# Macaron block (two mixture-of-experts layers around a selective scan): second expert layer of an older group in the first half of an iteration, first layer of a younger group in the second half

## The chip, the core and the metric

The kernel runs on one core of a Trainium2 chip. The metric is the device time of one execution in microseconds (us). The engines are PE (TensorE, matrix products), DVE (VectorE), ACT (ScalarE), POOL (GpSimd) and SP (SyncE, which here only issues DMAs). Each engine runs its own list of instructions in order, and they wait for each other through semaphores.

## What is computed

x holds 32 sequences of 256 tokens with 128 features. Three residual steps follow each other, each on the normalised result of the one before:

```
x = x + 0.5 * ffn(layernorm(x))
x = x + mamba(layernorm(x))
x = x + 0.5 * ffn(layernorm(x))
```

The expert layer `ffn` has 8 experts of width 176, of which each token takes two, and a shared part of width 352:

```
top_logits, idx = top_k(xf @ Wg, 2);  probs = softmax(top_logits);  w = scatter(probs)
h = silu(xf @ W1[e]) * (xf @ W2[e]);  y = sum_e w[:, e] * (h @ W3[e])
y = y + (silu(xf @ Ws1) * (xf @ Ws2)) @ Ws3
```

The middle step is a selective scan with 256 inner channels and 16 states:

```
x_in, z = split(x @ W_in + b_in);  x_conv = silu(conv4(x_in));  delta = softplus(x_conv @ W_dt + b_dt)
B, C = split(x_conv @ W_xp + b_xp)
h = exp(delta * A) * h + (delta * x_conv) * B;  y = sum_s h * C + D * x_conv
out = layernorm(x + (y * silu(z)) @ W_out + b_out) * alpha + beta
```

## The kernel before

**Groups and iterations.** Two sequences (512 tokens) form a group, and there are G = 16 groups. All tiles are 128 partitions by 512 tokens or twice that. The kernel is a software pipeline of iterations k. Iteration k scans group k (`scans`), prepares the scan of group k+1 (`lead`: `in0` to `in3`, the convolution, `dt0`, `dt1`, `xproj`, `delta`), begins group k+2 (`enters`: normalisation, routing and routing weights of the first expert layer) and finishes group k-1 (`tail`). Each iteration is cut into 32 slots. Every engine walks through the same slots (its own function `body(k, odd)`), so the order of all work is written out by hand.

**What stands in a slot.** Every even slot has one state of the scan on DVE (`hist`, L770), every odd slot the product for the next state (`dbx`, L733). POOL multiplies each finished state by its row of C (`prod`, L479), and for two states at a time issues a DMA that adds them to `yacc` in memory. ACT makes the decays of two states at once, four exponentials, in the slots of the table `DECAYS`: 0, 4, 8, 12, 16, 20 and 22, and for states 0 and 1 at the end of slot 31 (L569).

**The expert layers.** A layer has 14 chunks of 128 hidden channels (`NCHUNK`), one chunk per slot: in slot n PE multiplies for h1 and h2 of chunk n (L951, L966), ACT applies silu (L589), in slot n+1 DVE gates it (L757 and L779, or L754 for the three shared chunks), and in slot n+2 PE adds it to `ps_y` (L961). The result is copied (`yT`, ACT), transposed (PE) and added to `xres` (`addy`, DVE L837). `UP0 = 0` and `UP1 = 15` say where the layers start: the first layer of group k+1 goes through slots 0 to 15, the second layer of group k-1 through slots 15 to 30.

**The steps between.** The table `PLAN` places all else. A step is a name that several engines look for in the same slot: `conv1b` is two products on DVE (L855) and then a silu on ACT (`xconv`, L654); `dt1` is a product on PE (L1008), then Abs and Identity on ACT (L661, L663), the exponential (L667), and at the start of the next slot the logarithm (L579). All small products share one PSUM tile, `ps_m`, in turn (`turn`, `claim`, `take`). ACT has to load a table whenever it goes over from silu to exp or ln, or back (ACT_TABLE_LOAD). Within a slot ACT does first the silu of the slot's chunk, then the steps, then the decays.

**Tiles that carry a group.** `xres` holds XS = 4 groups. SP loads and stores them at the end of an iteration, behind the 7 loads of the C rows (`crow`).

## Time and profile before

| what | us |
|---|---|
| median of 3 runs | 2434.92 (2432.38 to 2435.53) |
| the profiled execution | 2431.15 |
| its span, first to last instruction | 2429.2 |
| up to the first state of the scan | 120.3 |
| iteration 0, from its first state to that of iteration 1 | 112.1 |
| iteration 6 (952.04 to 1096.78), the one shown below | 144.7 |
| iteration 15, to the end of its last state | 107.5 |
| after the last state | 89.3 |

The iterations are counted here from the first state of a scan to that of the next. A "pair" below is two slots, from one state of the scan to the next; pair 0 is slots 0 and 1, pair 15 is slots 30 and 31. In iteration 6 the 16 pairs begin at 952.04, 961.48, 969.19, 977.85, 985.33, 992.07, 998.87, 1007.52, 1014.41, 1028.38, 1037.75, 1048.48, 1061.69, 1071.45, 1080.21 and 1089.51 us. In the rows of windows below, behind the window and its length, stand the busy times of PE, PE's weight loads, DVE, ACT and POOL (with the number of instructions), the granted TensorE clock as a share of 2.4 GHz, DMA's share and GB/s. A window's length less the busy time of an engine is that engine's idle time in it.

### The profile page before, as it was taken

How to read it: one execution, taken by the hardware profiler on the slowest of the kernel's cores; microseconds unless marked ns; L12 is line 12 of the kernel's file. 1: busy time of each engine (PE TensorE's matmuls, PEld its weight loads, DVE VectorE, ACT ScalarE, POOL GpSimd, SP SyncE). 2: the span in 40 equal slices, each digit the busy share in tenths (PEclk: the TensorE clock that was granted, in tenths of full speed). 3: DMA queues.
4: the chain of work that ended last, by engine and by line, in shares of the span. 5: the costliest groups of instructions: out<-in, count | busy, mean ns of one | idle time of the engine just before them, and what ended most of it. 6: DMA issues, size and time to landing. Idle time of an engine off the chain costs nothing. (4 is left out here: it accounts for less than half of the span.)

```text
span 2429.2 us, 21997 instructions
## 1 busy us (share of the span) xinstructions
PE 1814.9 (75%) x4768; PEld 789.5 (32%) x4768; DVE 1877.2 (77%) x3077; ACT 1315.8 (54%) x1927; POOL 1071.5 (44%) x939
## 2 busy tenths in 40 slices
PE   4775787777778777788778777787877877785457
PEld 2332333333333333333333333333333333332123
DVE  2488878888887878887887888878878887887753
ACT  1465565555556555656556565655565655564422
POOL 3045635436263453635345363543636354363631
PEclk9695999899998999989989899989899999998688
DMA  2034323433343434334343433333434334344340
GB/s 76 18 80 111 93 65 94 99 84 92 73 101 73 105 78 104 78 79 102 80 98 85 96 87 79 91 91 79 104 87 94 70 87 104 74 104 100 87 91 5
DMA packets 62124, 206.45 MB, mean 85 GB/s; under 512 B 7648, under 2 KB 28864, under 8 KB 47680
## 3 DMA queue, kind: packets, MB, share of 16 engines
q0 software_dynamic: 18432, 125.84, 26.1%
q1 hardware_dynamic: 35840, 76.03, 9.6%
q10 hardware_dynamic: 7744, 3.57, 0.6%
q14 instruction: 93, 0.76, 0.1%
q8 instruction: 15, 0.25, 0.0%
...
## 5 line engine op out<-in xcount | busy, mean ns | idle before, releaser
L479 POOL TENSOR_TENSOR prod<-hist,crow 128x1024 f32<-128x1024 f32 x224 | 528.9, 2361 | 763.4 <-DVE hist L770 763.4
L770 DVE TENSOR_TENSOR_SCAN hist<-decay,dbx 128x1024 f32<-128x1024 f32 x256 | 625.0, 2441 | 24.6 <-ACT decay L569 21.1
L961 PE MATMUL ps_y<-gated,down_w 128*128 128x512 f32 (+1 forms) x896 | 497.8, 639 | 11.2 <-DVE gated L779 10.9
L569 ACT ACTIVATE decay<-delta,a_neg 128x510 f32<-128x510 f32 x512 | 326.6, 708 | 1.5
L733 DVE TENSOR_TENSOR dbx<-du,ps_bc 128x1024 f32<-128x1024 f32 x256 | 310.8, 1214 | 3.5 <-PE ps_bc L923 0.7
L589 ACT ACTIVATE silu<-ps_h1a 128x512 f32<-128x512 f32 (+1 forms) x224 | 132.8, 593 | 251.5 <-PE ps_h1a L951 247.3
L939 PE MATMUL ps_wb<-wT,sel_w 96*128 96x512 bf16 x352 | 138.9, 395 | 170.0 <-DVE gated L779 166.9
L951 PE MATMUL ps_h1b<-xnT,up_w 128*128 128x512 f32 x448 | 257.1, 658 | 10.8 <-ACT silu L589 10.7
L951 PE MATMUL ps_h1a<-xnT,up_w 128*128 128x512 f32 (+1 forms) x448 | 256.0, 655 | 12.0 <-ACT xnT L594 12.0
L923 PE MATMUL ps_bc<-bT,sel_b 96*128 96x512 bf16 x256 | 112.7, 440 | 200.8 <-DVE dbx L733 199.9
L966 PE MATMUL ps_h2a<-xnT,up_w 128*128 128x512 f32 (+1 forms) x448 | 253.5, 650 | 0.0
L961 PEld LDWEIGHTS ps_y<-gated,down_w 128*128 128x128 f32 (+1 forms) x896 | 176.2, 201 | 232.8 <-issue 190.7
L966 PE MATMUL ps_h2b<-xnT,up_w 128*128 128x512 f32 x448 | 239.6, 618 | 0.0
L779 DVE TENSOR_TENSOR gated<-silu,ps_wb 128x512 f32<-128x512 f32 x352 | 236.5, 672 | 1.3 <-PE ps_wb L939 0.6
L589 ACT ACTIVATE silu<-ps_h1b 128x512 f32<-128x512 f32 x224 | 133.5, 596 | 177.9 <-PE ps_h1b L951 177.0
L757 DVE TENSOR_TENSOR silu<-silu,ps_h2b 128x512 f32<-128x512 f32 x192 | 130.9, 682 | 93.6 <-ACT silu L589 51.1
L757 DVE TENSOR_TENSOR silu<-silu,ps_h2a 128x512 f32<-128x512 f32 x160 | 108.5, 678 | 115.2 <-ACT silu L589 63.2
L589 ACT ACT_TABLE_LOAD x136 | 174.5, 1283 | 10.7 <-PE ps_h1a L951 6.7
L569 ACT ACT_TABLE_LOAD x123 | 157.8, 1283 | 2.4 <-DVE delta L862 0.2
L939 PEld LDWEIGHTS ps_wb<-wT,sel_w 96*128 96x128 bf16 x352 | 37.4, 106 | 317.1 <-DVE gated L779 284.7
L966 PEld LDWEIGHTS ps_h2a<-xnT,up_w 128*128 128x128 f32 (+1 forms) x448 | 92.5, 207 | 125.6 <-issue 125.3
L966 PEld LDWEIGHTS ps_h2b<-xnT,up_w 128*128 128x128 f32 x448 | 92.0, 205 | 125.0 <-issue 124.7
...
## 6 DMA issues: line engine op xcount, KB each, us to landing
...
crow<-c_rows SPq DMA_DIRECT2D x128, 512.0 KB, 3.9
...
```

The lines of the kernel that those rows point to most:

```text
L479: nc.gpsimd.tensor_tensor(prod[:, (pair - 1 + odd) % 2, s % 2, :, :], hist[:, s % 2, :, :], c_all, ALU.mult).then_inc(prod_done, 1)
L569: ins = nc.scalar.activation(decay[:, s % NA, half, :, 1:LEN], d[:, :, 1:LEN], ACT.Exp, scale=a_neg[:, half, s:s + 1])
L589: nc.scalar.activation(silu[0:r, place, :], ps_h1[pos % 2][0:r, :], ACT.Silu).then_inc(silu_done, 1)
L733: nc.vector.tensor_tensor(dbx[:], du[par][:], ps_bc[:].unsqueeze(1).to_broadcast([P, HALVES, TG]), ALU.mult).then_inc(dbx_done, 1)
L757: nc.vector.tensor_tensor(silu[:, place, :], silu[:, place, :], ps_h2[pos % 2][:], ALU.mult).then_inc(mid_done, 1)
L770: nc.vector.tensor_tensor_scan(hist[:, s % 2, :, :].rearrange("p h t -> p (h t)"), decay[:, s % NA, :, :, :].rearrange("p h b t -> p (h b ...
L779: nc.vector.tensor_tensor(gated[:, place, :], silu[:, place, :], ps_wb[:], ALU.mult).then_inc(gate_done, 1)
L923: nc.tensor.matmul(ps_bc[:], sel_b[:, s, :], bT[par][:], start=True, stop=True).then_inc(b_full, 1)
L939: nc.tensor.matmul(ps_wb[:], sel_w[:, ORDER[pos], :], wT[f][:], start=True, stop=True).then_inc(wb_full, 1)
L951: nc.tensor.matmul(ps_h1[pos % 2][0:r, :], up_w[:, 0, j * P:j * P + r], xnT[f][:], start=True, stop=True).then_inc(h1_full, 1)
L961: nc.tensor.matmul(ps_y[:], down_w[0:rd, jd, :], gated[0:rd, (posd + NCHUNK * f_parity(k, fd)) % NSILU, :], start=(posd == 0), stop=(posd ...
L966: nc.tensor.matmul(ps_h2[pos % 2][0:r, :], up_w[:, 1, j * P:j * P + r], xnT[f][:], start=True, stop=True).then_inc(h2_full, 1)
```

## The change

The expert layers change their halves and their groups: slots 0 to 15 hold the second layer of group k-2 (a new condition `last`), slots 15 to 30 the first layer of group k+2 (`enters`). `xres` holds 5 groups, the pipeline has one more iteration (k = -2 to 17), and the loops and counters are adapted (`ffn_no`, `route_no`, `turn_last`, and `home`, which computes a group's place once). The steps move:

| steps | slots before | slots after |
|---|---|---|
| x1n, gate_y, outproj, outT, resid, stats3, ln_norm (group k-1) | 5, 3, 4, 5, 6, 7, 9 | 0, 5, 6, 8, 9, 10, 12 |
| stats1, norm1, xT1, logits1, route1, weights1, wT1 (group k-1) | 12, 13, 14, 15, 16, 17, 18 | 17, 18, 20, 21, 22, 24, 26 |
| stats0, norm0, xT0, logits0, route0, weights0, wT0 (group k+2) | 4, 10, 15, 18, 19, 24, 29 | 0, 2, 3, 4, 5, 7, 8 |
| stats2, norm2, xT2, in0, in1, in2, in3 (group k+1) | 17, 18, 19, 20, 21, 22, 23 | 1, 3, 5, 6, 7, 9, 10 |
| conv0a, conv0b, conv1a, conv1b, dt0, dt1 (group k+1) | 21, 22, 22, 23, 24, 25 | 7, 9, 10, 12, 14, 15 |
| xproj, bparts, cT, bT, delta (group k+1) | 26, 26, 27, 28, 28 | 18, 19, 22, 23, 25 |
| yT and addy, first layer / second layer | 16 / 31 | 31 / 16 |

`DECAYS` stays. The DMA that folds `yacc` moves from the end of slot 1 to slot 3 on POOL, SP stores and loads `xres` in the middle of the iteration, and each `statistics` gets a memset of one element.

ACT around the last step of the convolution (`xconv`), which follows slot 23 before:

```order
L654 ACTIVATE xconv<-dtmp,conv_b_c 128x512 [waits conv_ready]
L585 REGISTER_ALU
L589 ACTIVATE silu<-ps_h1b 128x512 [waits gate_done,h1_full]
L547 REGISTER_ALU
L661 ACTIVATE dtmp<-ps_m,b_dt_c 128x512 [waits misc_full]
```

and is in slot 12 now:

```order
L680 ACTIVATE xconv<-dtmp,conv_b_c 128x512 [waits conv_ready]
L581 ACTIVATE rtok<-rtok,nbiasr,stdr 128x128 [waits nbias_ready3]
L581 ACTIVATE rtok<-rtok,nbiasr,stdr 128x128 x3
L589 REGISTER_ALU
L594 ACT_TABLE_LOAD
L594 ACTIVATE decay<-delta,a_neg 128x2x255 [waits scan_done]
L594 ACTIVATE decay<-delta,a_neg 128x2x255
L589 REGISTER_ALU
L594 ACTIVATE decay<-delta,a_neg 128x2x255 [waits scan_done]
L594 ACTIVATE decay<-delta,a_neg 128x2x255
L611 REGISTER_ALU
L615 ACT_TABLE_LOAD [waits gate_done]
```

Before, the silu of a chunk (L589) comes right behind `xconv`; now four normalisations (`rtok`) and four decays with two table loads stand between them.

ACT at the end of `dt1` (exponential and logarithm into `dtmp`), slots 25 and 26 before:

```order
L667 ACT_TABLE_LOAD
L667 ACTIVATE dtmp<-dtmp 128x1024 [waits softplus_chain]
L579 ACT_TABLE_LOAD
L579 ACTIVATE dtmp<-dtmp 128x1024 [waits softplus_chain]
L585 REGISTER_ALU
L589 ACT_TABLE_LOAD [waits gate_done]
L589 ACTIVATE silu<-ps_h1b 128x512 [waits h1_full]
```

and slots 15 and 16 now:

```order
L693 ACT_TABLE_LOAD
L693 ACTIVATE dtmp<-dtmp 128x1024 [waits softplus_chain]
L605 ACT_TABLE_LOAD
L605 ACTIVATE dtmp<-dtmp 128x1024 [waits softplus_chain]
L611 REGISTER_ALU
L613 REGISTER_ALU [waits h1_full]
L615 ACT_TABLE_LOAD
L615 ACTIVATE silu<-ps_h1b 128x512 [waits gate_done]
L660 ACTIVATE yT<-ps_y 128x512 [waits down_done]
```

The copy `yT` of the finished layer stands right behind that stretch now. On DVE the slots 15 and 16 are now the product `dbx`, one gate, one state of the scan and then the addition of the finished layer (`xres<-ps_m`):

```order
L760 TENSOR_TENSOR dbx<-du,ps_bc 128x1024 [waits scan_done,b_full]
L777 ISA
L781 REGISTER_ALU [waits h2_full,silu_done]
L782 TENSOR_TENSOR gated<-silu,ps_h2a 128x512 [waits down_done]
L798 SCALAR_TENSOR_TENSOR hist<-decay,dbx 128x1024 [waits prod_done,decay_ready,dbx_done]
L863 REGISTER_ALU
L865 ISA [waits misc_full]
L865 SCALAR_TENSOR_TENSOR xres<-ps_m,xres 128x512
L777 REGISTER_ALU
L781 REGISTER_ALU [waits h2_full,silu_done]
L782 TENSOR_TENSOR gated<-silu,ps_h2b 128x512 [waits down_done]
```

Before, the routing of the other layer (`route1`) stood between the scan and that addition.

The diff, cut to its core:

```diff
     PLAN = {
...
-        23: ["in3", "conv1b"], 24: ["dt0", "weights0"], 25: ["dt1"], 26: ["xproj", "bparts"],
+        9: ["resid", "in2", "conv0b"], 10: ["in3", "stats3", "conv1a"], 12: ["conv1b", "ln_norm"], 14: ["dt0"],
+        15: ["dt1"], 16: ["yT1", "addy1"], 17: ["stats1"], 18: ["norm1", "xproj"], 19: ["bparts"], 20: ["xT1"],
     }
-    UP0, UP1 = 0, 15
+    UP1, UP0 = 0, 15
 
     DECAYS = {0: 2, 4: 4, 8: 6, 12: 8, 16: 10, 20: 12, 22: 14}
 
-    MISC_ENTRY = ["xT0", "logits0", "wT0"]
-    MISC_LEAD = ["yT0", "xT2", "in0", "in1", "in2", "in3", "dt0", "dt1", "xproj", "cT", "bT"]
-    MISC_TAIL = ["outproj", "outT", "xT1", "logits1", "wT1", "yT1"]
+    MISC_ENTRY = ["xT0", "logits0", "wT0", "yT0"]
+    MISC_LEAD = ["xT2", "in0", "in1", "in2", "in3", "dt0", "dt1", "xproj", "cT", "bT"]
+    MISC_TAIL = ["outproj", "outT", "xT1", "logits1", "wT1"]
+    MISC_LAST = ["yT1"]
+
+    FULL = 2
...
     def ffn_no(k, f):
 
+        if isinstance(k, int) and k < FULL:
+            return k + 2
+        if isinstance(k, int) and k >= G - 2:
+            return k + G - 2
+        return 2 * k + 1 - f
+
+    def route_no(k, step):
+
         if isinstance(k, int) and k < 1:
-            return k + 1
-        if isinstance(k, int) and k >= G - 1:
-            return 2 * (G - 1) + (k - (G - 1))
-        return 2 * k + f
-
-    def route_no(k, step):
-
-        return ffn_no(k, 1) if step.endswith("1") else ffn_no(k + 1, 0)
+            return k + 2
+        if isinstance(k, int) and k >= G - 2:
+            return k + G - 1
+        return 2 * k + (2 if step.endswith("1") else 1)
...
     def up_unit(k, slot):
 
-        if UP0 <= slot < UP0 + NCHUNK and lead(k):
+        if UP0 <= slot < UP0 + NCHUNK and enters(k):
             return 0, slot - UP0
-        if UP1 <= slot < UP1 + NCHUNK and tail(k):
+        if UP1 <= slot < UP1 + NCHUNK and last(k):
             return 1, slot - UP1
         return None
...
     def iterations(engine, body):
 
-        body(-2, 0)
-        body(-1, 1)
-        body(0, 0)
-        with engine.Fori(1, G - 3, 2) as k:
-            body(k, 1)
-            body(k + 1, 0)
-        for k in range(G - 3, G + 1):
+        for k in range(-2, FULL):
+            body(k, k % 2)
+        with engine.Fori(FULL, G - 2, 2) as k:
+            body(k, 0)
+            body(k + 1, 1)
+        for k in range(G - 2, G + 2):
             body(k, k % 2)
...
-        XS = 4
+        XS = 5
...
             def rows_c(g, par, p):
 
+                if p == 0:
+                    sp.wait_ge(misc_taken, turn(g - 1, "cT"))
+                    sp.dma_start(c_rows[par, :, :], cT[:]).then_inc(c_stored, 16)
                 if p > 1 or not isinstance(g, int) or g > 0:
                     sp.wait_ge(prod_done, NS * g + 2 * p - 2)
                 if p == 0:
-                    sp.wait_ge(misc_taken, turn(g - 1, "cT"))
-                    sp.dma_start(c_rows[par, :, :], cT[:]).then_inc(c_stored, 16)
                     sp.wait_ge(c_stored, 16 * (g + 1))
                 sp.dma_start(crow[:, (p % 2) * 2:(p % 2) * 2 + 2, :],
                              c_rows[par, 2 * p:2 * p + 2, :].partition_broadcast(P)).then_inc(crow_ready[p % 2], 16)
 
             def body(k, odd):
                 if scans(k):
-                    for p in range(1, NS // 2):
+                    for p in range(1, NS // 4 + 2):
+                        rows_c(k, odd, p)
+                if last(k):
+                    at, stored, loaded = home(sp, k - 2), row_of(k - 2), row_of(k - 2 + XS)
+                    store(k - 2, at, stored, k)
+                    if not isinstance(k, int) or k - 2 + XS < G:
+                        load(k - 2 + XS, at, loaded)
+                if scans(k):
+                    for p in range(NS // 4 + 2, NS // 2):
                         rows_c(k, odd, p)
                 if lead(k):
                     rows_c(k + 1, 1 - odd, 0)
-                if tail(k):
-                    store(k - 1, (k - 1) % XS, k)
-                    if not isinstance(k, int) or k - 1 + XS < G:
-                        load(k - 1 + XS, (k - 1) % XS)
 
...
                         elif step == "stats2" and lead(k):
+                            if tail(k):
+                                pool.wait_ge(x1n_ready, k)
...
+                        elif step == "fold" and tail(k):
+                            pool.wait_ge(acc_done, 16 * PAIRS * k)
+                            ticket((PAIRS + 1) * (k - 1) + PAIRS)
+                            pool.dma_start(yacc[nxt][:, 0, :, :], yacc[nxt][:, 1, :, :], accum_op=ALU.add
+                                           ).then_inc(folded, 16)
...
-                    if slot == 1 and tail(k):
-                        pool.wait_ge(acc_done, 16 * PAIRS * k)
-                        ticket(8 * k - 1)
-                        pool.dma_start(yacc[nxt][:, 0, :, :], yacc[nxt][:, 1, :, :], accum_op=ALU.add
-                                       ).then_inc(folded, 16)
...
             def statistics(src, which, agg, number):
 
                 chain = Chain(dve, dve_stats, 1, number)
+                nc.vector.memset(carrier_s[:], 0.0)
...
-                        elif step == "yT0" and lead(k) or step == "yT1" and tail(k):
+                        elif step == "yT0" and enters(k) or step == "yT1" and last(k):
                             pass
-                        elif step == "addy0" and lead(k) or step == "addy1" and tail(k):
+                        elif step == "addy0" and enters(k) or step == "addy1" and last(k):
                             f = int(step[4])
                             dve.wait_ge(misc_full, turn(k, f"yT{f}"))
-                            xr = xres[:, behind if f else ahead, :, :].rearrange("p t c -> p (t c)")
+                            xr = xres[:, oldest if f else entering, :, :].rearrange("p t c -> p (t c)")
                             nc.vector.scalar_tensor_tensor(xr, ps_m[:], 0.5, xr, ALU.mult, ALU.add
                                                            ).then_inc(misc_taken, 1)
                         elif step in ("conv0a", "conv1a") and lead(k):
```

## Rows read from the trace of the kernel before

**Rows 1.** The page's part 1: busy time, share, instructions of the engines.

```profile
PE 1814.9 (75%) x4768; PEld 789.5 (32%) x4768; DVE 1877.2 (77%) x3077; ACT 1315.8 (54%) x1927; POOL 1071.5 (44%) x939
```

**Rows 2.** Windows of five stretches: length, busy time by engine, TensorE's clock, DMA.

```profile
35.86:80.45 44.59, 42.19 (x105) 18.40 (x103) 19.03 (x35) 12.85 (x22) 1.55 (x4) 1.00 0.00 1
120.35:174.88 54.53, 42.40 (x101) 16.85 (x100) 43.44 (x51) 32.65 (x45) 21.95 (x16) 0.97 0.31 73
174.88:232.44 57.56, 27.12 (x75) 11.88 (x73) 50.61 (x68) 32.78 (x45) 32.11 (x23) 0.59 0.48 110
378.61:2096.22 1717.61, 1349.73 (x3577) 588.98 (x3576) 1406.01 (x2304) 995.09 (x1453) 784.73 (x685) 0.92 0.38 89
...
2339.90:2429.20 89.30, 48.94 (x126) 21.72 (x124) 27.68 (x75) 15.65 (x30) 13.68 (x20) 0.79 0.11 24
```

**Rows 3.** Windows of iteration 6, pairs 0, 6, 7, 8, 10, 13, 15, sum.

```profile
952.04:961.48 9.44, 7.98 (x16) 2.79 (x14) 4.71 (x4) 9.11 (x12) 3.75 (x4) 0.85 0.96 218
...
998.87:1007.52 8.65, 6.04 (x16) 2.40 (x15) 8.61 (x16) 7.20 (x11) 7.24 (x8) 1.00 0.58 142
1007.52:1014.41 6.89, 5.34 (x20) 2.45 (x18) 5.79 (x6) 1.96 (x4) 4.17 (x4) 1.00 0.25 50
1014.41:1028.38 13.97, 10.57 (x30) 4.87 (x30) 9.72 (x42) 8.62 (x13) 5.86 (x8) 0.88 0.50 113
...
1037.75:1048.48 10.73, 10.27 (x27) 4.28 (x25) 7.02 (x9) 8.00 (x12) 2.37 (x1) 1.00 0.28 57
...
1071.45:1080.21 8.76, 8.29 (x36) 4.64 (x35) 7.12 (x14) 6.80 (x8) 3.44 (x3) 1.00 0.22 45
...
1089.51:1096.78 7.27, 6.51 (x12) 3.01 (x12) 4.20 (x4) 4.43 (x6) 3.44 (x3) 0.50 0.17 46
sum 144.74, PE 114.35 PEld 49.93 DVE 117.64 ACT 83.96 POOL 66.25; mean PE 7.15 PEld 3.12 DVE 7.35 ACT 5.25 POOL 4.14
```

**Rows 4.** Timeline, ACT: start, length; silu of the convolution in slot 22, what follows it.

```profile
1054.56 0.72 ACT L654 ACTIVATE xconv<-dtmp,conv_b_c 128x512 f32<-128x512 f32 x1 [4.24 <-DVE dtmp L855]
...
1056.60 2.55 ACT L569 ACTIVATE decay<-delta,a_neg 128x510 f32<-128x510 f32 x4
...
1060.46 0.60 ACT L589 ACTIVATE silu<-ps_h1a 128x512 f32<-128x512 f32 x1
...
1136.73 1.64 ACT L556 ACTIVATE rtok<-rtok,nbiasr,stdr 128x128 f32<-128x128 f32 x4
```

**Rows 5.** Timeline, PE and ACT: step dt1 from its product to the next silu.

```profile
1067.42 1.88 PE L1008 MATMUL ps_m<-xconv,w_dt 128*128 128x512 f32 x4
...
1069.33 0.69 ACT L661 ACTIVATE dtmp<-ps_m,b_dt_c 128x512 f32<-128x512 f32 x1 [2.84 <-PE ps_m L1008]
...
1070.62 1.28 ACT L667 ACT_TABLE_LOAD   x1
1071.91 1.06 ACT L667 ACTIVATE dtmp<-dtmp 128x1024 f32<-128x1024 f32 x1
...
1076.65 0.60 ACT L589 ACTIVATE silu<-ps_h1b 128x512 f32<-128x512 f32 x1
```

**Rows 6.** Timeline: copy, transposes and addition of a finished layer, iteration 6, slot 16.

```profile
1020.60 0.59 ACT L634 ACTIVATE yT<-ps_y 128x512 f32<-128x512 f32 x1
...
1021.32 0.66 PE L915 MATMUL ps_m<-ident,yT 128*128 128x128 f32 x4 [0.47 <-ACT yT L634]
...
1022.01 0.69 DVE L837 SCALAR_TENSOR_TENSOR xres<-ps_m,xres 128x512 f32 x1 [3.61 <-PE ps_m L915]
```

**Rows 7.** The page's part 5: DVE's work of a slot with a chunk.

```profile
L733 DVE TENSOR_TENSOR dbx<-du,ps_bc 128x1024 f32<-128x1024 f32 x256 | 310.8, 1214 | 3.5 <-PE ps_bc L923 0.7
L779 DVE TENSOR_TENSOR gated<-silu,ps_wb 128x512 f32<-128x512 f32 x352 | 236.5, 672 | 1.3 <-PE ps_wb L939 0.6
```

**Rows 8.** Two DVE lines by themselves: durations ns min/median/max of all their instructions.

```profile
L862 DVE SCALAR_TENSOR_TENSOR delta<-dpre,dtmp x16: 1200/3022/3026, 114.3 to 2220.8; 128x1024 f32<-128x1024 f32 x16
...
L855 DVE SCALAR_TENSOR_TENSOR dtmp<-xin,conv_w_c,dtmp x64: 727/752/2714, 91.4 to 2196.6; 128x512 f32<-128x512 f32 x64
```

More of the change, by code:

```diff
@@ L78, in tail, with last @@
     def tail(k):
-        return not isinstance(k, int) or k >= 1
+        return not isinstance(k, int) or 0 <= k - 1 < G
+    def last(k):
+        return not isinstance(k, int) or 0 <= k - 2 < G
     def misc_list(k):
-        names = (enters(k) * MISC_ENTRY) + (lead(k) * MISC_LEAD) + (tail(k) * MISC_TAIL)
+        names = (enters(k) * MISC_ENTRY) + (lead(k) * MISC_LEAD) + (tail(k) * MISC_TAIL) + (last(k) * MISC_LAST)
         return [n for s in range(SLOTS) for n in PLAN.get(s, []) if n in names]
@@ L88, in before @@
             return sum(len(names_of(i)) for i in range(-2, k))
-        return sum(len(names_of(i)) for i in range(-2, 1)) + (k - 1) * len(names_of(1))
+        return sum(len(names_of(i)) for i in range(-2, FULL)) + (k - FULL) * len(names_of(FULL))
     def turn(k, name):
@@ L318, in _, with row_of, load, store @@
         def _(sp):
-            def load(g, slot):
+            def row_of(g):
+                return g * NSEQ if isinstance(g, int) else sp.snap(g * NSEQ)
+            def load(g, slot, first):
                 sp.dma_start(xres[:, slot, :, :],
-                             x[bass.ds(g * NSEQ, NSEQ)].rearrange("b (t p) c -> p (b t) c", p=P)).then_inc(x_loaded, 16)
-            def store(g, slot, k):
+                             x[bass.ds(first, NSEQ)].rearrange("b (t p) c -> p (b t) c", p=P)).then_inc(x_loaded, 16)
+            def store(g, slot, first, k):
                 sp.wait_ge(misc_taken, turn(k, "yT1"))
                 sp.wait_ge(x_loaded, 16 * min(g + XS, G) if isinstance(k, int) else 16 * (g + XS))
-                sp.dma_start(out[bass.ds(g * NSEQ, NSEQ)].rearrange("b (t p) c -> p (b t) c", p=P),
+                sp.dma_start(out[bass.ds(first, NSEQ)].rearrange("b (t p) c -> p (b t) c", p=P),
                              xres[:, slot, :, :]).then_inc(x_stored, 16)
@@ L348, in body @@
                     rows_c(k + 1, 1 - odd, 0)
-                if tail(k):
-                    store(k - 1, (k - 1) % XS, k)
-                    if not isinstance(k, int) or k - 1 + XS < G:
-                        load(k - 1 + XS, (k - 1) % XS)
             for g in range(XS):
-                load(g, g)
+                load(g, g, row_of(g))
                 sp.wait_ge(x_loaded, 16 * (g + 1))
-            body(-1, 1)
-            body(0, 0)
-            with sp.Fori(1, G - XS - 1, 2) as k:
-                body(k, 1)
-                body(k + 1, 0)
-            for k in range(G - XS - 1, G + 1):
+            for k in range(-1, FULL):
+                body(k, k % 2)
+            with sp.Fori(FULL, G - XS - 1, 2) as k:
+                body(k, 0)
+                body(k + 1, 1)
+            for k in range(G - XS - 1, G + 2):
                 body(k, k % 2)
@@ L438, in body @@
                 nxt = 1 - odd
-                behind = (k - 1) % XS if tail(k) else 0
+                behind = home(pool, k - 1) if tail(k) else 0
                 for slot in range(SLOTS):
@@ L574, in body @@
                 nxt = 1 - odd
-                entering, ahead, behind = (k + 2) % XS, (k + 1) % XS, (k - 1) % XS if tail(k) else 0
+                entering, ahead = home(act, k + 2), home(act, k + 1)
+                behind = home(act, k - 1) if tail(k) else 0
                 for slot in range(SLOTS):
@@ L739, in body @@
                 nxt = 1 - odd
-                entering, ahead, behind = (k + 2) % XS, (k + 1) % XS, (k - 1) % XS if tail(k) else 0
+                entering, ahead = home(dve, k + 2), home(dve, k + 1)
+                behind, oldest = home(dve, k - 1) if tail(k) else 0, home(dve, k - 2) if last(k) else 0
                 for slot in range(SLOTS):
@@ L992, in body @@
                             to_rows(bparts, KP, ident_bf, ps_m[:, 0:TG // 2].bitcast(BF16)).then_inc(misc_full, 1)
-                        elif step == "yT0" and lead(k) or step == "yT1" and tail(k):
+                        elif step == "yT0" and enters(k) or step == "yT1" and last(k):
                             f = int(step[2])
```

20 lines of the change are left out of this document (11 added, 9 removed), and 8 rows, old and new, of the table PLAN.

## The prediction, made before the changed kernel was run

> **What bounds the kernel now.** I read the busy shares first. DVE is the busiest engine with 1877.2 us of 2429.2 [rows 1], so an iteration is DVE's own work plus the time in which DVE waits. Then I read the windows of one iteration, cut at the starts of the scan's states. In iteration 6 DVE works 117.6 of 144.7 us and waits 27.1 us [rows 3]; over iterations 2 to 13 the mean length is 1717.6 / 12 = 143.1 us [rows 2]. The waits are not spread evenly: 4.7 us stand in pair 0 (9.44 less 4.71), none in pair 6, 1.1 us in pair 7, 4.3 us in pair 8, 1.6 us in pair 13 [rows 3]. What they have in common is seen in the timeline of ACT. ACT is busy for 84 of 144.7 us only [rows 3], but it is in order, and a burst of decays or of exp and ln makes the next silu late, for which DVE's gate of the next chunk waits, with the scan's next state behind it in DVE's queue. Whatever the change does, it counts by what it does to these waits, and by what one more iteration costs at the ends.
>
> **The change, first in a full iteration.** No product, gate or scan is added or removed; the same 28 chunks lie beside 16 states. What moves is what DVE has to do while ACT runs its bursts.
>
> *Slot 12, new wait.* conv1b now ends slot 12 on DVE, and ACT has behind it xconv, then the four normalisations of ln_norm, then decays, and only then the silu of the last chunk. Before, xconv in slot 22 had the decays behind it: from the start of xconv (1054.56) to the end of the silu (1061.06) it took 6.5 us, and the normalisations take 1.64 us [rows 4]. With 0.1 us for the release that is 8.2 us from the end of conv1b to the silu. DVE meanwhile has slot 13: two gates of some 0.67 us and a dbx of 1.21 us [rows 7], 2.4 us as they overlap a little. So DVE stands for 8.2 - 2.4 = 5.8 us ahead of state 7. In slot 22 the same chain was covered, since conv1a and conv1b followed on DVE. Pair 6 has no idle time now: +5.8 us.
>
> *Slots 15 and 16, longer wait.* Here the finished layer is added, and dt1 now stands in the way. From the end of slot 14's gate PE has a product into ps_y and one for h2 (1.9 us together) and dt1's product (1.9 us), then ACT needs from the start of Abs (1069.33) to the end of the next silu (1077.25) 7.9 us [rows 5], and from the start of yT (1020.60) to the addition (1022.01) it is 1.4 us [rows 6]. Sum 13.1 us. DVE has in it one dbx, one gate and one state, 4.0 us, so it stands 9.1 us, and about 1 us more for the silu behind the decays of slot 16. Before, pairs 7 and 8 together wait 1.1 + 4.3 = 5.4 us [rows 3]; the routing that filled this place is in slot 22 now. 10.1 - 5.4 = +4.7 us.
>
> *Pair 0.* x1n is put on ACT between a silu and the decays of slot 0, which makes the next silu later by 1.6 us (the same four normalisations as in [rows 4]); stats0 and stats2 give DVE 2.4 us to do in the 4.7 us that it waits there [rows 3]: -0.8 us.
>
> *The other waits.* 27.1 less 4.7, 5.4 us is 17.0 us in 13 pairs. Those of pair 10 (decays behind a copy, 10.73 us with 7.02 of work, 3.7 us) and pair 15 (a layer's addition and the first decays, 7.27 with 4.20, 3.1 us) [rows 3] stand unchanged in the new order. Of the other 10.2 us a large part is owed to short chains that now have slots between them: xproj to bparts (pair 13, 1.6 us), the transposes, the convolution. I take 6.5 us away; the ends are 0 and 10.
>
> *DVE against POOL.* delta takes 3.0 us in the iterations and 1.2 us where POOL is idle, and a step of the convolution up to 2.7 instead of 0.75 us [rows 8], where they start while POOL's product with C runs, that is in an even slot right behind a state. delta goes from slot 28 to 25 (-1.8 us), conv0b from 22 to 9 (-1.8 us), conv1a is beside POOL's stats3 (+0.5 us); the weights step in slot 24 stays one in an even slot. -3.1 us. Ends: -4 and 0.
>
> *TensorE's clock.* In the windows with gaps of PE it is granted at half (0.50, 1.2 GHz) or partly, 0.88 in pair 8 [rows 3]. The two longer waits leave PE idle too, for 6 us before the ps_y product and 5 us before the transposes. I take +2 us, between 0 and 5.
>
> Together +5.8 + 4.7 - 0.8 - 6.5 - 3.1 + 2.0 = +2.1 us, for 12 iterations with both layers **+25 us**. The memsets (64 of 0.06 us) and the fold DMA, which gets two more slots than it needs and no longer holds POOL, I cost at nothing: they lie in POOL's idle time and between DVE's waits. SP's store and load now stand ahead of the C rows of states 12 and 13, behind the addition of slot 16; these rows are wanted in slot 24, some 30 us later, so this is nothing as long as the store's landing takes a few us.
>
> A rule of the Trainium skill speaks against the change more than my rows do. In [rows 5] the table load of 1.28 us starts at 1070.62 and the exponential at 1071.91: nothing stands between them, and the next silu follows its load as closely. The Trainium skill, ScalarE: Activation LUTs, section What ACT_TABLE_LOAD costs, states about 1.38 us of drain beside each load of 1.28 us. With it the stretch of slot 12 (two loads) would be 2.8 us and that of slot 15 (three loads) 4.1 us longer, and the sum for 12 iterations some 80 us higher. The row decides, and I leave it out.
>
> **The ends.** A layer in the clear takes 44.6 us, from its first product to its addition [rows 2]. What follows from it at the ends are estimates. *Head:* group 1's layer now runs before the first state. +44.6, + 13 for steps that get in line ahead of it and bursts within it, less 16 us of dt1 to delta that now run beside it (dt1's stretch alone is 9.8 us, 1067.42 to 1077.25 [rows 5], and the transposes of B and C follow): +42. *Tail:* one more layer, + 44.6, + 10 for the steps between its chunks, less 34 us of fold to ln_norm, which now run beside it (89.3 less 44.6 us [rows 2] are 44.7 us for all that stands ahead of the last layer, and stats1 to xT1 keep some 11 of them), + 3 for routing steps that lay beside the layer: +24. *Iterations with one layer:* before 0 and 15, now 0, 1, 14 and 15. Before, these two and two full ones are 112.1 + 107.5 + 286.2 = 506 us (the first two as in the table above, the full ones by [rows 2]). Now I put together halves: iteration 0 is a half of scan and lead steps without a layer (57.6) and one with a layer and the new wait (54.5 + 9) [rows 2], 121 us; iteration 1 the same with the tail's steps, 131; iteration 14 a full first half without steps of an entering group, 68, and some 50 for scans with steps; 15 a layer and tail steps, 61, and bare scans, 41. Together 472 us, -34. The ends come to 42 + 24 - 34 = **+32 us**, between +10 and +55.
>
> **The sum.** The profiled execution took 2431.15 us (span 2429.2 us). 2431.15 + 25 + 32 = 2488 us. The median of the runs is 3.8 us above that execution, so 2492 us.
>
> **Rivals.** *The new waits are covered* (for the change). If ACT's queue is not as far behind as I put it, so that both silus come in time, an iteration is 10.5 us shorter than in my sum, -8.4 instead of +2.1: -101 + 32 gives 2366 us. It needs both; with one of them covered, 5.3 us less on the average, it is 2428 us. For it speaks that all chains get more slots and that 27 us of waits are there to be won. Against it, the order of ACT is fixed and the two stretches are read from it: DVE has 2.4 and 4.0 us of work for 8.2 and 13.1 us. It decides at 2.7 us less per iteration than I have, where the gain pays for the ends. *PE becomes slow in the gaps* (against): if PE is granted half its clock from slot 14 to slot 19, as it is in pair 15 (0.50) [rows 3], a chunk takes PE 6.0 us instead of 3.0 (14 chunks in 42.19 us at the full clock [rows 2]), more than DVE's 2.4 to 3.5 us of a slot; two slots of that beyond what I took are 5 us per iteration: + 60, 2552 us. *The ends alone*: all waits even out, no change per iteration, 2431 + 32, with the median 2467 us; this lies in my range.
>
> **Chances.** Forecast, slower by 1 to 4 % (with the ends-alone case): 0.58. PE slow: 0.17. One wait covered: 0.10. Both covered: 0.15. So that no more than 2 in 10 are left out, the range goes from 2395 us, below the case of one covered wait, to 2555 us: what is left out is most of the both-covered case and the far end of the slow one. This kernel's measurement can tell about 0.2 % from no change. The one-wait case lies on both sides of that line: faster 0.22, within 0.2 % 0.04, slower 0.74.
>
> **What will show it.** The windows of a full iteration: pair 6 should be near 14 us (8.65 before), with DVE waiting for a silu ahead of state 7; pair 8 near 16 us with DVE's addition waiting for PE's transposes 8 us and POOL idle; pairs 9, 11 and 13 shorter than before, pair 12 longer, as weights1 and delta are both there. First state near 162 us, 113 us after the last. DVE's busy time should fall by some 35 us over the kernel through delta and the convolution. I am wrong in the first place if pair 6 or pair 8 shows no wait for ACT; then the silu came earlier than the order of ACT allows by my reading. I am wrong in the ends if the first state starts before 150 us.

## The result, and the profile after

| | before | changed |
|---|---|---|
| median of the runs, us | 2433.65 (2430.09 to 2435.53) | 2502.39 (2500.11 to 2504.03) |
| ratio | | 1.0284, 95% interval 1.0266 to 1.0301 |
| span of the profiled execution | 2429.2 | 2502.3 |
| up to the first state | 120.3 | 160.7 |
| iterations 0 and 1 | 112.1, 146.2 | 114.7, 128.9 |
| iterations 2 to 13, mean | 143.1 | 146.9 |
| iterations 14 and 15 | 136.2, 107.5 | 125.4, 105.1 |
| after the last state | 89.3 | 104.2 |

The changed kernel is 2.8 % slower; the forecast was 2492 us. Of the 73.1 us by which the span grew, 40.4 are in the head, 14.9 in the tail, 12 times 3.8 = 45.7 in iterations 2 to 13, and -27.9 in iterations 0, 1, 14 and 15. All four of these lack one layer in the changed kernel; before, only 0 and 15 did.

The page's part 1 and windows of four stretches of the changed kernel (length, busy time of PE, weight loads, DVE, ACT, POOL, TensorE's clock, DMA), which answer to [rows 1, 2]:

```profile
PE 1807.3 (72%) x4768; PEld 794.9 (32%) x4768; DVE 1839.2 (74%) x3141; ACT 1301.0 (52%) x1916; POOL 1110.4 (44%) x939
```

```profile
0.00:160.74 160.74, 108.78 (x276) 49.52 (x276) 57.49 (x156) 44.66 (x71) 26.89 (x43) 0.89 0.14 37
160.74:275.40 114.66, 70.32 (x175) 29.88 (x175) 94.03 (x121) 60.48 (x86) 52.85 (x38) 0.74 0.37 88
404.33:2167.59 1763.26, 1331.64 (x3578) 585.26 (x3577) 1349.38 (x2353) 994.25 (x1453) 808.26 (x685) 0.91 0.37 86
2398.09:2502.30 104.21, 83.56 (x212) 37.56 (x212) 44.38 (x102) 21.18 (x38) 13.75 (x20) 0.91 0.10 22
```

DVE works less than before, 1839.2 us instead of 1877.2. In the twelve full iterations its work fell by (1406.0 - 1349.4) / 12 = 4.7 us and its waits grew by 8.5 us, from 26.0 to 34.5 us. Where the waits stand is seen in the windows of iteration 6 (pairs 0, 6 to 11, 13, 15, and the whole), against [rows 3]:

```profile
992.61:1002.85 10.24, 7.04 (x15) 2.54 (x13) 6.95 (x24) 9.86 (x15) 5.87 (x10) 0.89 0.67 152
...
1043.62:1058.49 14.87, 11.04 (x23) 4.10 (x21) 9.06 (x10) 9.21 (x15) 10.76 (x7) 0.89 0.45 106
1058.49:1065.99 7.50, 4.58 (x6) 2.00 (x7) 4.60 (x6) 1.01 (x2) 3.54 (x4) 0.58 0.26 68
1065.99:1082.57 16.58, 9.95 (x23) 4.40 (x22) 6.47 (x16) 14.10 (x17) 3.59 (x4) 0.78 0.37 84
1082.57:1089.39 6.82, 6.82 (x31) 3.99 (x30) 6.50 (x12) 2.77 (x6) 5.70 (x5) 1.00 0.24 77
1089.39:1099.17 9.78, 9.52 (x33) 4.64 (x31) 5.79 (x7) 7.40 (x10) 2.36 (x1) 1.00 0.60 127
1099.17:1109.83 10.66, 6.98 (x23) 3.13 (x23) 7.39 (x23) 6.94 (x10) 4.71 (x5) 1.00 0.21 64
...
1121.97:1130.08 8.11, 5.53 (x16) 2.53 (x15) 5.79 (x8) 1.19 (x2) 3.44 (x3) 0.79 0.29 78
...
1135.18:1139.91 4.73, 2.81 (x9) 1.30 (x10) 4.10 (x4) 3.40 (x5) 2.35 (x1) 1.00 0.00 0
992.61:1139.91 147.30, 109.64 (x298) 48.41 (x297) 112.42 (x196) 81.82 (x120) 65.50 (x56) 0.92 0.37 86
```

Length less DVE's busy time is DVE's wait: 5.8 us in pair 6, where there was none; 2.9 and 10.1 in pairs 7 and 8, where it was 1.1 and 4.3. The timeline shows what ends them (start, length, engine, line, operation; in brackets the idle time before it and what ended it). DVE first:

```profile
1048.26 1.53 DVE L883 SCALAR_TENSOR_TENSOR dtmp<-xin,conv_w_c,dtmp 128x512 f32<-128x512 f32 x2
...
1057.88 0.69 DVE L785 TENSOR_TENSOR silu<-silu,ps_h2b 128x512 f32<-128x512 f32 x1 [5.77 <-ACT silu L615]
...
1065.38 0.69 DVE L782 TENSOR_TENSOR gated<-silu,ps_h2a 128x512 f32<-128x512 f32 x1 [2.90 <-PE ps_h2a L994]
...
1077.53 0.69 DVE L865 SCALAR_TENSOR_TENSOR xres<-ps_m,xres 128x512 f32 x1 [9.26 <-PE ps_m L943]
```

and ACT in the same 30 us (slots 12 to 16):

```profile
1049.82 0.72 ACT L680 ACTIVATE xconv<-dtmp,conv_b_c 128x512 f32<-128x512 f32 x1 [4.78 <-DVE dtmp L883]
1050.45 1.63 ACT L581 ACTIVATE rtok<-rtok,nbiasr,stdr 128x128 f32<-128x128 f32 x4
1052.10 1.28 ACT L594 ACT_TABLE_LOAD   x1
1053.39 2.55 ACT L594 ACTIVATE decay<-delta,a_neg 128x510 f32<-128x510 f32 x4
1055.96 1.28 ACT L615 ACT_TABLE_LOAD   x1
1057.26 0.60 ACT L615 ACTIVATE silu<-ps_h1b 128x512 f32<-128x512 f32 x1
...
1067.68 0.69 ACT L687 ACTIVATE dtmp<-ps_m,b_dt_c 128x512 f32<-128x512 f32 x1 [8.18 <-PE ps_m L1036]
...
1074.99 0.60 ACT L615 ACTIVATE silu<-ps_h1b 128x512 f32<-128x512 f32 x1
1075.48 0.59 ACT L660 ACTIVATE yT<-ps_y 128x512 f32<-128x512 f32 x1
```

From the end of conv1b (1049.79) to the end of the silu (1057.86) it is 8.1 us; the prediction had 8.2. From the start of Abs (1067.68) to the end of the next silu (1075.59) it is 7.9 us, as before the change [rows 5], and only then comes the copy `yT`, for which PE's transposes and DVE's addition wait. ACT, with 52 % of the span busy, sets the end of the waits of pairs 6 and 8; in pair 8 it had itself waited 8.2 us for PE's product of dt1.

### The profile page after: what moved, and what is told of

Same layout as the page of the kernel before. It is cut to its first block, busy times and chain, and to the rows that moved or that the text cites. A ratio compares the mean times of both kernels' runs of the same rounds, so it can differ in the third digit from the quotient of the medians.

```text
span 2502.3 us, 22059 instructions
## 1 busy us (share of the span) xinstructions
PE 1807.3 (72%) x4768; PEld 794.9 (32%) x4768; DVE 1839.2 (74%) x3141; ACT 1301.0 (52%) x1916; POOL 1110.4 (44%) x939
## 4 chain that ended last, share of the span: by engine, by line
PE 34%; issue 23%; ACT 16%; DVE 15%; POOL 7%; DMA 4%; DVEq 1%; ACTq 0%; POOLq 0%
PE ps_y L989 8%; ACT decay L594 4%; PE ps_h1a L979 4%; PE ps_h2a L994 4%; DVE hist L798 3%; PE ps_h2b L994 3%; DVE gated L807 3%; PE ps_h1b L979 3%; ACT L594 3%; ACT L615 3%; PE ps_m L1036 2%; POOL prod L509 2%; DMA yacc<-yacc 2%; PE ps_wb L967 2%; PE ps_m L943 2%
## 5 line engine op out<-in xcount | busy, mean ns | idle before, releaser
L509 POOL TENSOR_TENSOR prod<-hist,crow 128x1024 f32<-128x1024 f32 x224 | 538.5, 2404 | 616.0 <-DVE hist L798 615.0
L989 PE MATMUL ps_y<-gated,down_w 128*128 128x512 f32 (+1 forms) x896 | 507.0, 650 | 79.1 <-DVE gated L807 76.6
L979 PE MATMUL ps_h1b<-xnT,up_w 128*128 128x512 f32 x448 | 245.2, 630 | 19.8 <-ACT silu L615 19.8
L443 POOL TENSOR_TENSOR varp<-mv,ln_eps 128x4 f32<-128x4 f32 x32 | 10.3, 323 | 282.2 <-DVE mv L729 282.2
```

What stands on the lines that cost most here:

```text
L509: nc.gpsimd.tensor_tensor(prod[:, (pair - 1 + odd) % 2, s % 2, :, :], hist[:, s % 2, :, :], c_all, ALU.mult).then_inc(prod_done, 1)
L979: nc.tensor.matmul(ps_h1[pos % 2][0:r, :], up_w[:, 0, j * P:j * P + r], xnT[f][:], start=True, stop=True).then_inc(h1_full, 1)
L989: nc.tensor.matmul(ps_y[:], down_w[0:rd, jd, :], gated[0:rd, (posd + NCHUNK * f_parity(k, fd)) % NSILU, :], start=(posd == 0), stop=(posd ...
```

## The experiments

**The theory (A):** what costs is ACT's fixed order. A burst of decays (four exponentials between two table loads, 5.1 us) or of exponential and logarithm stands between a copy or silu that waits for DVE or PE and the next chunk's silu, so DVE waits for nearly the whole burst. **Rivals:** (B) PE's pace and clock set these pairs, ACT is only the last to show it; (C) the loss lies in the head and tail alone, full iterations even out. Each kernel below was timed beside the kernel before on the same chip. Each edit is small and leaves every product in place, except where said.

**e1: the burst of slot 12 in slot 11.**

```diff
-    DECAYS = {0: 2, 4: 4, 8: 6, 12: 8, 16: 10, 20: 12, 22: 14}
+    DECAYS = {0: 2, 4: 4, 8: 6, 11: 8, 16: 10, 20: 12, 22: 14}
```

> Changed kernel (2502 us) with one number of DECAYS moved: the decays of states 8 and 9 in slot 11 instead of 12, so that ACT no longer has them (4.5 us with two table loads) between conv1b's silu and the silu of slot 13's chunk. Theory A (ACT's fixed order makes the waits of pair 6 and, with it, the long iterations): pair 6 falls from 14.9 us to 10 to 11 us, an iteration by 3.5 to 5 us, the kernel by 45 to 65 us, to about 2445 us. Rival B (PE's pace and clock set pairs 6 to 8): pair 6 shortens but pairs 7 and 8 take it back, 0 to -20 us in all, 2482 to 2502 us. Rival C (the ends alone are the loss, full iterations even out): no change, 2502 us.

Measured: 2410.86 us, ratio to before 0.9908 (0.9891 to 0.9924). One number of a table turns 2.8 % slower into 0.9 % faster. B (20 us less at most) and C (no change) are out for this burst. The gain is also more than A had: 1679.63 / 12 = 140.0 us per full iteration, 7.0 us less. Pairs 6, 7 and 8 of iteration 6 and the twelve full iterations, then two of PE's products behind slot 14:

```profile
1015.55:1025.14 9.59, 6.89 (x17) 2.60 (x16) 9.07 (x9) 5.23 (x9) 5.80 (x4) 1.00 0.64 150
1025.14:1032.54 7.40, 7.17 (x18) 3.05 (x17) 4.79 (x5) 2.39 (x5) 7.08 (x5) 1.00 0.09 18
1032.54:1046.80 14.26, 7.63 (x18) 3.43 (x18) 8.52 (x16) 13.94 (x17) 8.53 (x7) 0.76 0.54 133
402.54:2082.17 1679.63, 1298.97 (x3578) 572.67 (x3577) 1382.18 (x2352) 994.02 (x1453) 849.23 (x685) 0.94 0.38 90
```

```profile
1029.13 1.02 PE L994 MATMUL ps_h2a<-xnT,up_w 128*128 128x512 f32 x2
1029.98 1.88 PE L1036 MATMUL ps_m<-xconv,w_dt 128*128 128x512 f32 x4
```

In the changed kernel the same two groups read:

```profile
1063.27 1.91 PE L994 MATMUL ps_h2a<-xnT,up_w 128*128 128x512 f32 x2
1064.98 2.66 PE L1036 MATMUL ps_m<-xconv,w_dt 128*128 128x512 f32 x4
```

So the wait of pair 6 was paid twice: 5 us as such, and then again in pairs 7 and 8, because PE, held up with DVE, started the product of dt1 late and at half clock (0.58 in pair 7, 1.00 now). DVE's waits in pairs 7 and 8 fell from 13.0 to 2.6 + 5.7 = 8.3 us. Part of the clock that B speaks of is real: in pair 7 it follows from ACT's burst, in pair 8 it stayed (0.78, now 0.76). And part of the gain goes back, so that the two pairs together are only 2.4 us shorter (24.1 to 21.7): states that used to start while POOL stood still now start beside its product. POOL and DVE at state 8:

```profile
1030.06 4.66 POOL L509 TENSOR_TENSOR prod<-hist,crow 128x1024 f32<-128x1024 f32 x2
```

```profile
1032.55 4.33 DVE L798 TENSOR_TENSOR_SCAN hist<-decay,dbx 128x1024 f32<-128x1024 f32 x1 [1.52 <-POOL prod L509]
```

The scan, 2.28 us in most places, begins at 1032.55 while POOL works until 1034.72, and ends 2.16 us after that. Nearly its whole length lies behind POOL's work, so in this row it stood still and did not merely run slower beside it. The Trainium skill, SBUF — State Buffer, section SBUF: two separate sides, says that a DVE operation with two SBUF inputs and a GpSimd operation that reads SBUF take a shared pair of ports as an exclusive lock for a whole instruction, whichever starts first. The row agrees.

**e2: ln_norm in slot 13.**

```diff
-        9: ["resid", "in2", "conv0b"], 10: ["in3", "stats3", "conv1a"], 12: ["conv1b", "ln_norm"], 14: ["dt0"],
+        9: ["resid", "in2", "conv0b"], 10: ["in3", "stats3", "conv1a"], 12: ["conv1b"], 13: ["ln_norm"], 14: ["dt0"],
```

> Changed kernel with ln_norm (four normalisations on ACT, 1.64 us, and two products on POOL) in slot 13 instead of 12. Theory A: silu of slot 13's chunk stands behind 1.6 us less on ACT's list, pair 6 falls by about 1.6 us, the next pair takes some of it back; kernel -10 to -21 us, about 2485 us. Rival B (PE's pace): 0 to -5 us. Rival C (ends alone): no change.

Measured: 2500.07 us, ratio to before 1.0273 (1.0256 to 1.0290), the changed kernel 1.0284: nearly nothing, a miss for the number of A. The mechanism is there all the same. The wait in pair 6 fell from 5.8 to 4.3 us (15.91 - 11.64), while DVE's work in it grew by 2.6 us:

```profile
1040.32:1056.23 15.91, 11.33 (x23) 3.88 (x21) 11.64 (x10) 7.68 (x11) 7.15 (x4) 0.89 0.41 99
```

```profile
1044.97 4.09 DVE L883 SCALAR_TENSOR_TENSOR dtmp<-xin,conv_w_c,dtmp 128x512 f32<-128x512 f32 x2
```

```profile
1045.05 2.66 POOL L509 TENSOR_TENSOR prod<-hist,crow 128x1024 f32<-128x1024 f32 x1
```

These two products of conv1b took 1.53 us above. In the changed kernel POOL stood waiting for the normalisations of ln_norm at that time and began its product 12.6 us after the state's start (1056.24 after 1043.62); now it begins 4.7 us after it, and conv1b stands beside it. Thus removing a wait of POOL moved a conflict onto DVE. The twelve full iterations say the same: DVE waits 30.5 us of each instead of 34.5, and works 116.1 us instead of 112.4. This agrees with A on the wait but, as a time, can't be told from B.

**e3: exponential and logarithm of dt1 behind `yT`.**

```diff
-                    if "dt1" in PLAN.get(slot - 1, []) and lead(k):
-                        act.wait_ge(softplus_chain, (HALVES + 1) * (k + 2))
-                        nc.scalar.activation(dtmp[:], dtmp[:], ACT.Ln, bias=1.0).then_inc(logterm_ready, 1)
...
-                            if half == HALVES - 1:
-                                act.wait_ge(softplus_chain, (HALVES + 1) * (k + 2) - 1)
-                                nc.scalar.activation(dtmp[:], dtmp[:], ACT.Exp, scale=-1.0
-                                                     ).then_inc(softplus_chain, 1)
+                    late = "dt1" in PLAN.get(slot - 1, []) and lead(k)
+                    if late:
+                        act.wait_ge(softplus_chain, (HALVES + 1) * (k + 2) - 1)
+                        nc.scalar.activation(dtmp[:], dtmp[:], ACT.Exp, scale=-1.0).then_inc(softplus_chain, 1)
                     if slot == SLOTS - 1 and lead(k):
                         decays(k + 1, nxt, range(NA // 2))
                     elif slot in DECAYS and scans(k):
                         decays(k, odd, range(DECAYS[slot], DECAYS[slot] + 2))
+                    if late:
+                        act.wait_ge(softplus_chain, (HALVES + 1) * (k + 2))
+                        nc.scalar.activation(dtmp[:], dtmp[:], ACT.Ln, bias=1.0).then_inc(logterm_ready, 1)
```

> Changed kernel with ACT's exponential of dt1 moved behind the copy yT of the finished layer (end of slot 16) and the logarithm behind the decays of that slot, which also saves two table loads. Theory A: the addition in pair 8 waits about 3 us for PE's transposes instead of 7.4 us, part of it comes back where the next silu stands behind exp, decays and ln (wait 1.5 us becomes 4 to 5 us); net -2 to -4 us per iteration, kernel 2455 to 2475 us. Rival B (PE's clock and pace in the gap): pair 8 stays at 16 us, kernel 2495 to 2505 us. Rival C: no change.

Measured: 2444.07 us, ratio 1.0042 (1.0026 to 1.0059), 58 us less than the changed kernel and 11 us below A's range. Pair 8 fell from 16.6 to 13.4 us, with TensorE at the full clock (0.78 before), as the window of pair 8 and rows of ACT and DVE show:

```profile
1042.20:1055.64 13.44, 11.18 (x42) 5.62 (x40) 6.47 (x17) 11.97 (x16) 3.93 (x5) 1.00 0.56 129
```

```profile
1045.23 0.59 ACT L657 ACTIVATE yT<-ps_y 128x512 f32<-128x512 f32 x1
...
1054.32 0.59 ACT L612 ACTIVATE silu<-ps_h1a 96x512 f32<-96x512 f32 x1
```

```profile
1046.83 0.69 DVE L865 SCALAR_TENSOR_TENSOR xres<-ps_m,xres 128x512 f32 x1 [2.35 <-PE ps_m L943]
...
1055.03 0.68 DVE L782 TENSOR_TENSOR gated<-silu,ps_h2a 96x512 f32<-96x512 f32 x1 [4.58 <-ACT silu L612]
```

The addition waits 2.4 us instead of 9.3, the gate behind it 4.6 instead of 0.8: theory A's exchange. B had pair 8 unchanged and is out for this pair. The edit also saves 28 table loads (ACT has 1888 instructions instead of 1916), so part of the 58 us may be theirs; e6 below has the same edit without that saving. The iterations give 12 x 3.5 = 42 us; the other 16 come from the head and iterations 0, 1 and 14, which have the same stretch.

**e7: only the two late bursts.** Slots 20 and 22 also have a copy that waits (`xnT`, `cT`), a burst, then a silu.

```diff
-    DECAYS = {0: 2, 4: 4, 8: 6, 12: 8, 16: 10, 20: 12, 22: 14}
+    DECAYS = {0: 2, 4: 4, 8: 6, 12: 8, 16: 10, 21: 12, 24: 14}
```

> Changed kernel (2502 us) with only the two late bursts of decays moved (20 to 21, 22 to 24); slots 12 and 16 as they were. It prices the waits of pairs 10 and 11 that I had not foreseen. Theory A: pairs 10 and 11 shorten by 2.8 us each, 5.6 us per full iteration and less in the others, 2420 to 2435 us. Rival B (PE's pace takes it back in pairs 12 to 15): 2460 to 2500 us.

Measured: 2410.82 us, ratio 0.9905 (0.9889 to 0.9922), -92 us, 9 us below A's range; B is out. Pairs 10 and 11 are 3.2 and 2.95 us shorter and nothing comes back:

```profile
1052.98:1059.58 6.60, 6.42 (x26) 3.48 (x25) 5.79 (x8) 3.56 (x5) 2.35 (x1) 1.00 0.87 185
1059.58:1067.29 7.71, 7.49 (x27) 3.52 (x26) 7.30 (x24) 5.60 (x9) 3.75 (x4) 1.00 0.00 1
```

**e4: all four bursts moved** (12 to 11, 16 to 17, 20 to 21, 22 to 24).

> Changed kernel with four numbers of DECAYS moved (12 to 11, 16 to 17, 20 to 21, 22 to 24), so that no burst of four exponentials with its two table loads stands between a copy that waits and the silu of a chunk. Theory A: pair 6 -4.6 us, pair 8 -1 us, pair 10 -3.5 us, pair 11 -2.6 us, about -11 us per full iteration, kernel about 2350 to 2380 us, below the kernel before (2434 us). Rival B (PE's clock and pace set the length of an iteration): -20 to -40 us in all, 2462 to 2482 us. Rival C (only the ends were lost, full iterations even out): 2495 to 2505 us.

Measured: 2332.44 us, ratio 0.9584 (0.9568 to 0.9600), -170 us against the changed kernel. That is less than e1 and e7 together (-92 and -92), so the gains don't simply add up. Part of it is the move of slot 16: over the full iterations, pair 8 is 0.25 us shorter than in e1 (15.40 to 15.15) and pair 9, behind slot 17, 1.0 us longer (6.6 to 7.6). The time lies 18 us below A's range, far beyond B's and C's.

**e5 and e9: the same tables in the kernel before.** e5 is the kernel before with e4's table, e9 with e7's.

> Control: the kernel before (2434 us), its order untouched, with the table of decays that took the changed kernel from 2502 to 2332 us (12 to 11, 16 to 17, 20 to 21, 22 to 24). Theory A (what counts is which copy and which silu stand around a burst, so a table belongs to its order): before, only the burst of slot 20 stands behind a copy that waits (in0) and ahead of a silu that DVE waits for (3.35 us in pair 10, and 0.6 us in pair 11); it gives -3 to -4 us per iteration, 2375 to 2400 us, so that the changed order keeps an advantage of 40 us or more. Rival D (the new table is simply better in any order, the change of order brings nothing): before falls to 2332 us or below.

> Control: kernel before (2434 us) with only the two late bursts of decays moved (20 to 21, 22 to 24), the edit that gave the changed kernel -92 us. With all four moved, the kernel before won 5.4 us in pairs 10 and 11 and lost 5.2 us in pairs 1, 9, 12 and 13. Theory A1 (pair 9's loss of 1.7 us and pair 1's of 1.2 us come from the burst moved from slot 16 to 17, the rest from the late ones): 2.4 us less per iteration, 2400 to 2410 us. Theory A2 (the order of before leaves PE no slack there, so that a wait won in pair 10 returns in the pairs around it, whichever burst is moved): 2420 to 2432 us.

Measured: e5 2424.84 us, ratio 0.9959 (0.9944 to 0.9973), a miss for A (2375 to 2400) though the changed order keeps a lead of 92 us and D, which wanted 2332 us or less, is out; e9 2391.37 us, 0.9824 (0.9808 to 0.9840), so A1's side (2400 to 2410) and beyond, not A2's. e9's windows of pairs 10 to 13, where [rows 3] have 10.73 for pair 10 and 8.76 for pair 13:

```profile
1023.71:1030.81 7.10, 7.10 (x19) 3.05 (x18) 7.01 (x9) 2.24 (x4) 2.37 (x1) 1.00 0.40 82
1030.81:1042.36 11.55, 10.24 (x26) 4.19 (x25) 11.44 (x14) 9.24 (x13) 3.87 (x3) 1.00 0.50 126
1042.36:1052.85 10.49, 9.05 (x23) 3.66 (x22) 9.53 (x18) 8.34 (x13) 2.34 (x1) 1.00 0.07 13
1052.85:1062.98 10.13, 7.54 (x35) 4.34 (x34) 7.85 (x13) 8.02 (x9) 3.44 (x3) 1.00 0.35 72
```

The same edit is worth 43 us there and 92 us in the changed order. Pairs 10 and 11 give 5.3 us and then pairs 12 and 13 take 2.1 back, probably because before the change slot 24 has routing weights and dt0 around the burst; this was not tried. The 33 us between e9 and e5 come from the bursts moved to slots 11 and 17. Pair 9, behind slot 17, is 2.3 us longer per iteration in e5 than in e9, so most of it should be the one in 17; that one alone was not tried. A table of bursts belongs to the order around it.

**e6 and e8: what both changes of ACT's order give.** e6 is e3's edit and e4's table; e8 also moves the burst of slot 0 to slot 1, where it stands behind the silu of that slot's chunk instead of ahead of it.

> Changed kernel with both edits: the four moved bursts of decays (alone 2332 us) and the exponential and logarithm of dt1 behind the copy yT (alone -58 us). Theory A: the wait of the addition in pair 8 (4.5 us left) falls by 2 to 3 us per iteration, so 2290 to 2315 us; if exp, ln and the decays now collide in slots 16 and 17, the gate waits for them and it gives nothing (2325 to 2340 us). Rival B (PE's clock and pace set pair 8): no change against 2332 us.

> As the kernel with both edits (four moved bursts, exponential and logarithm behind yT), and the burst of slot 0 in slot 1 as well, where it no longer stands between x1n and the silu of slot 1's chunk, for which the gate waits 3.1 us. Theory A: pair 0 shortens by 2 to 3 us, 25 to 45 us less than with both edits, 2255 to 2290 us. Rival: the decays of state 2 come too late for slot 4 or pair 1 and 2 take it back (no change against both edits).

Measured: e6 2285.27 us, ratio 0.9393 (0.9377 to 0.9408); e8 2259.22 us, 0.9277 (0.9262 to 0.9293). e6 is 47 us faster than e4, 5 us below A's range, and B (no change) is out. e6 has as many table loads as e4 (ACT has 1916 instructions in both), so what e3's edit gives there is the order and not a saved load. e8 lies in A's range and is 174 us faster than the kernel before, with the same products, gates and states. Against e6, pair 0 fell from 9.9 to 6.9 us in iteration 6, but pair 1 grew from 4.5 to 5.5, so part of it came back. Pairs 0 and 8 and the sum of iteration 6 of e8:

```profile
905.93:912.84 6.91, 5.62 (x11) 2.10 (x10) 6.82 (x24) 6.80 (x11) 3.29 (x6) 0.79 0.96 220
...
971.90:982.37 10.47, 9.78 (x34) 4.57 (x32) 8.40 (x15) 9.50 (x11) 8.87 (x8) 1.00 0.65 152
...
sum 128.88, PE 107.52 PEld 47.29 DVE 117.05 ACT 81.54 POOL 68.60; mean PE 6.72 PEld 2.96 DVE 7.32 ACT 5.10 POOL 4.29
```

DVE now waits 11.8 of 128.9 us; DVE itself is the bound. Its work rose from 112.4 to 117.1 us: POOL works 68.6 us of the 128.9 instead of 65.5 of 147.3, and more states and products start beside it (a state takes 2.61 us on the average of the kernel, 2.46 in the changed one).

**g10: ten groups instead of sixteen,** for both kernels; it tells what is paid once from what is paid per iteration. Both kernels then leave out the last 12 sequences, so only their times are of use.

```diff
-    G = BATCH // NSEQ
+    G = 10
```

> Kernel before with 10 groups instead of 16: the last 12 sequences are left out, head, tail and the iterations with one layer stay. It has six full iterations fewer at 143.1 us each: 2434 - 859 = 1575 us by every theory.

> Changed kernel with 10 groups instead of 16 (the last 12 sequences are left out). Theory (the loss has a fixed part of about 27 us at the two ends and a part of 3.8 us in each full iteration): six full iterations fewer at 146.9 us: 2502 - 881 = 1621 us, 46 us more than the kernel before with 10 groups, where it is 69 us more with 16. Rival C (the ends alone): 69 us more here as well, 1644 us. Rival F (the loss is all in the full iterations, the ends cancel): 69 times 6 / 12, about 34 us more, 1609 us.

Measured: 1573.01 us (1571.12 to 1574.90) and 1622.61 us (1620.32 to 1625.69). The difference is 49.6 us, with 16 groups it is 68.7. So 19 us hang on six full iterations, 3.2 us each by the medians, and some 30 us are paid once. C wanted 69 here, and the rival that puts all into the iterations 34: both are out. The six full iterations, 3.9 us apart each in the profiled executions:

```profile
380.82:1238.81 857.99, 674.55 (x1789) 294.53 (x1788) 705.01 (x1152) 497.64 (x727) 393.01 (x343) 0.92 0.38 89
```

```profile
405.78:1286.89 881.11, 672.60 (x1790) 294.80 (x1789) 675.22 (x1176) 497.25 (x727) 404.83 (x343) 0.91 0.36 86
```

## Why the prediction was right, point by point

- **The forecast** (2492 us, 2395 to 2555, slower) held: 2502.4 us, 10 us beyond it. The ends and the full iterations have the predicted signs; e1 and e3 show the cause named, ACT's order, by removing it, and e7 shows it at two places that were not named. The number came out as near as this partly by luck: the sum had the full iterations 21 us too low and the ends 5 us too high, and the span grew by 73.1 us, but the median by 68.7 only.
- **Slot 12, +5.8 us per iteration:** 5.8 us, by the chain that was summed (8.1 us, predicted 8.2). e1 removes it.
- **Slots 15 and 16, +4.7 us:** pairs 7 and 8 wait 13.0 us where 10.1 were expected, +7.7. The chain on ACT was right to a tenth (7.9 us); the term was too small because it took PE at the full clock from slot 14's gate on. From the end of that gate (1061.35) to Abs (1067.68) PE's three products took 6.3 us, predicted 3.8. With the +2.0 that stood apart for the clock it is 6.7 against 7.7. e1 shows that the low clock of pair 7 was the first wait's after-effect.
- **Pair 0, -0.8 us:** 4.7 to 3.3 us, -1.4 in iteration 6; -0.5 on the average of the twelve (4.2 to 3.7).
- **The other waits, -6.5 us:** what is left of the sum of iteration 6 is 34.9 - 27.1 - 5.8 - 7.7 + 1.4 = -4.3 us. This is the term that was wrong in kind and not in size alone. The gains came in pairs 1, 2, 4, 5, 9 and 15 (pair 15 from 3.1 to 0.6, though it was to stay unchanged), but the wait of pair 11 went from 1.7 to 3.3 us, and that of pair 13 from 1.6 to 2.3 in the iteration shown (1.65 to 1.39 on the average). In slot 22 the burst now stands behind `cT`, which waits for PE's transposes, and ahead of a silu. That is exactly the pattern of slot 12, and the order of ACT showed it; I had looked for it at the two largest places only. e7 prices pairs 10 and 11 together at 92 us (pair 10 had its part of that before as well).
- **DVE against POOL, -3.1 us:** -4.7 us. delta takes 1.22 us in all 16 groups (3.02 us in most before [rows 8]), and the 64 products of the convolution 0.80 on the average instead of 1.16.
- **Per full iteration +2.1 us:** +3.8, so +45.7 in place of +25 us. Waits were 3.3 us too low, work 1.6 us too high.
- **The ends, +32 us:** +27.4. Head +40.4 (+42 predicted). Tail +14.9 (+24): the size was off, and no run here tells which of its terms. The four iterations with one layer fewer take 474.1 us (472), but the 506 us that they were set against are 502.0: iterations 1 and 14 are not two average full ones.
- **The table loads:** the drain of 1.38 us beside each load, stated in the Trainium skill, ScalarE: Activation LUTs, section What ACT_TABLE_LOAD costs, would have added some 80 us to the sum, 2572 us. The measured 2502 and the rows speak against it here: the load at 1052.10 takes 1.28 us and the exponential starts at 1053.39.
- **The rivals:** "both waits covered" and "one covered" did not happen; both stand in the rows. "PE slow from slot 14 to 19" happened in part, in pairs 7 and 8 alone (0.58, 0.78; 1.00 in pair 9). "The ends alone" is refuted by g10. One line of the working is wrong: the gain pays for the ends at -2.7 us per iteration, which is 4.8 us less than the sum's +2.1 and not 2.7.
- **The signs named:** pair 6 14.9 us (near 14), pair 8 16.6 (near 16), pairs 9, 11 and 13 shorter, pair 12 longer (12.1 against 9.8), DVE's work 38 us less (35), first state at 160.7 (162), but 104 us after the last and not 113.

The one thing that neither sum nor rivals had in view is how cheaply the waits could be undone. The rivals had a case with both waits covered at 2366 us; four numbers of `DECAYS` gave 2332. The theory behind the experiments was too careful as well: e1, e3, e4, e6 and e7 all gained more than it said, and only e2, and e5 in the other order, gained less.
